# Graph layers on one core: products of the early y blocks move into the first stage

## The chip, the cores and the metric

The kernel runs on one core of a Trainium2 chip. The metric is the device time of the launch in microseconds, the median of the runs; lower is better. TensorE (PE), VectorE (DVE), ScalarE (ACT), GpSimd (POOL) and SyncE (SP) run their own instruction streams and meet at semaphores.

## The reference

6250 nodes with 128 features, 200,000 edges sorted by their target `dst`, and 128 attributes on every edge. Two layers, cut to what matters:

```
h = relu(layernorm(x));  xp = h @ W                      # 4 heads of 32
e = leaky_relu(a_s[src] + a_d[dst]);  m = segment_max(e, dst)
alpha = exp(e - m[dst]) / segment_sum(exp(e - m[dst]), dst)
x = x + relu(segment_sum(alpha * xp[src], dst) + bias)   # loops included

h = relu(layernorm(x));  edge_agg = segment_sum(attr @ We + be, dst)
x_comb = [h, edge_agg];  neigh = segment_sum(x_comb[src], dst)
x = x + relu((x_comb + neigh) @ W1 + b1) @ W2 + b2
```

The second layer's sum over neighbours is linear, so the kernel projects first: y = x_comb @ W1 (one row of 128 per node), and needs z = y + A y, where A counts the edges from each source to each target.

## The kernel before

**First stage.** The edges are taken in 87 groups of 2304 (18 columns of 128), some 72 target rows each; a group's window is the 128 rows from its first target on. `item(n, b, it)` exists for each engine and handles group n with buffers b = n mod 2; `pairs` and `groups` unroll two groups in a loop body. In one group POOL gathers 18 x 128 rows of a table by `src` (L816). DVE reads the logits from them (L1638), scans for segment maxima (L1643, L1664), builds one-hot selections; TensorE merges the peaks (L1161), looks up shifts (L1177), sums attributes (L1133) and, once DVE has scaled the gathered rows V (L1742), sums V (L1194). DVE and ScalarE finish the window of the group before in between (layernorm, projection to y), and SyncE stores it to `sums1`.

Beside it the kernel builds A. For each of a group's 18 columns TensorE makes an adjacency pair: two products of one-hot edge marks (L1123 and L1125) into one of three PSUM banks, which ScalarE copies to `adjE[b]` (`keep_adjacency`, L905, shown as L852). Columns 0 to 2, 3 to 5 and so on stand at fixed places between the other work; columns 9 to 14 stand behind the V products, 15 to 17 in the next group. `adjE[b]` holds, for the group's 128 target rows, a 128 x 49 table: sources are split in 49 blocks of 128 (`adjT[b][:, :, h]` is the block h, with sources on the partitions). SyncE stores it to `adj` in DRAM one group later (`store_adjacency`). Each engine runs its list in order; SyncE's list is written out by hand in `item`, L540 on.

**Second stage.** When all is stored, SyncE loads y from `sums1` in four chunks (`YCH`) and DVE and ScalarE split every block into three bf16 parts side by side (`y_part`), giving `yb` with 384 columns a block. Then 49 windows of 128 rows: SyncE loads the window's adjacency (three buffers, `load_adjacency`, 1568 KB), TensorE accumulates 49 products of 384 columns (L1248), DVE reduces the three parts (L1799) and adds y's own rows, loaded by `load_z` into `state` (L1803). TensorE transposes the window before at product 16 and projects it at product 32 (`transpose_z`, `project_z`), ScalarE applies the relu, DVE adds the residual (L1792), SyncE stores the output.

Behind it stands a general path for inputs whose rows a group's window doesn't cover (`uncovered`, from `flag`); it does not run for these inputs.

## Time and profile before

| | us |
|---|---|
| median of 3 runs (lowest, highest) | 3118.07 (3117.33, 3122.89) |
| profiled execution, its own time | 3102.13 |
| its span | 3100.2 |
| PE busy / DVE / ACT / POOL | 2043.0 / 1807.2 / 1085.6 / 1673.2 |
| mean granted TensorE clock | 0.764 |

Busy shares are means over the whole span, and the two stages differ, so most of what is read below is by stretch. In the slices a digit is a tenth of a slice of 77.5 us. Granted clock 1.00 stands for 2.4 GHz, 0.50 for 1.2 GHz, values between for a stretch that holds both. Times in a timeline are from the span's start.

### The profile page before, as it was taken

How to read it: one execution, taken by the hardware profiler on the slowest of the kernel's cores; microseconds unless marked ns; L12 is line 12 of the kernel's file. 1: busy time of each engine (PE TensorE's matmuls, PEld its weight loads, DVE VectorE, ACT ScalarE, POOL GpSimd, SP SyncE). 2: the span in 40 equal slices, each digit the busy share in tenths (PEclk: the TensorE clock that was granted, in tenths of full speed). 3: DMA queues.
4: the chain of work that ended last, by engine and by line, in shares of the span. 5: the costliest groups of instructions: out<-in, count | busy, mean ns of one | idle time of the engine just before them, and what ended most of it. 6: DMA issues, size and time to landing. Idle time of an engine off the chain costs nothing.

```text
span 3100.2 us, 64216 instructions
## 1 busy us (share of the span) xinstructions
PE 2043.0 (66%) x16208; PEld 1674.9 (54%) x16208; DVE 1807.2 (58%) x6198; ACT 1085.6 (35%) x2295; POOL 1673.2 (54%) x1626
## 2 busy tenths in 40 slices
PE   4365665665665655665656656656656656699998
PEld 3354554554554544554545545545545544588887
DVE  7566676665666666666666766766766766411111
ACT  3134344344434443443443443443444443300000
POOL 4566666666666666666666666666666666000000
PEclk8677777776777767777767777777777777799999
DMA  9855655655655555655556556556556555666654
GB/s 192 134 163 177 194 168 174 195 159 180 193 155 187 177 169 189 189 160 185 162 176 194 157 184 194 168 173 194 156 185 194 156 185 176 225 213 214 225 212 146
DMA packets 276907, 560.29 MB, mean 181 GB/s; under 512 B 113395, under 2 KB 211139, under 8 KB 248081
## 3 DMA queue, kind: packets, MB, share of 16 engines
q1 hardware_dynamic: 226763, 444.37, 42.5%
q0 software_dynamic: 50112, 115.56, 16.5%
q8 instruction: 12, 0.20, 0.0%
q14 instruction: 20, 0.16, 0.0%
HBM read 382.53 MB, written 177.22 MB: 181 GB/s over the span
## 4 chain that ended last, share of the span: by engine, by line
PE 41%; issue 20%; DVE 15%; DMA 9%; another core or an unknown queue 5%; SPq 3%; ACT 2%; POOL 2%; ACTq 1%; DVEq 1%; POOLq 0%
PE pv L1133 10%; PE pv L1248 9%; DMA big<-table,idx 8%; PE pv L1194 7%; PE pt L1248 4%; PE pt L1123 3%; PE pm L1161 2%; POOL big L816 2%; ACT xsb L852 2%; PE pa L1123 1%; DVE peaks L1513 1%; DVE tabb L1477 1%; PE pa L1177 1%; ACTq L905 1%
## 5 line engine op out<-in xcount | busy, mean ns | idle before, releaser
L816 POOL DMA_INDIRECT big<-table,idx x1566 | 1639.8, 1047 | 929.9 <-issue 414.2
L852 ACT ACTIVATE xsb<-pt 128x343 f32 x1042 | 477.8, 459 | 1213.3 <-PE pt L1125 567.1
L1133 PE MATMUL pv<-big 128*128 128x128 f32 x3132 | 523.6, 336 | 5.7 <-ACT big L852 3.5
L1133 PEld LDWEIGHTS pv<-big 128*128 128x128 f32 x3132 | 490.3, 246 | 36.1 <-issue 11.7
L1123 PE MATMUL pt<-tabb 128*128 128x343 bf16 x1042 | 400.0, 384 | 65.8 <-ACT xsb L852 36.5
L1194 PE MATMUL pv<-big 128*128 128x133 f32 x3132 | 391.3, 280 | 7.0 <-DVE big L1742 4.2
L1638 DVE COPY logit<-big 128x72 f32<-128x72 f32 x87 | 21.9, 252 | 608.6 <-DMA big<-table,idx 540.1
L1194 PEld LDWEIGHTS pv<-big 128*128 128x128 f32 x3132 | 367.8, 190 | 16.2 <-DVE big L1742 8.6
L1477 DVE TENSOR_TENSOR tabb<-iotah,keyp 128x2064 bf16<-128x2064 bf16 x261 | 319.7, 1225 | 0.0
L1142 PE MATMUL pm<-ident,pre 128*4 128x128 f32 x87 | 32.5, 374 | 433.9 <-DVE pre L1643 226.5
L1248 PE MATMUL pv<-big,xsb 128*128 128x384 bf16 (+1 forms) x1617 | 279.3, 330 | 18.5 <-DVE big L1779 18.5
L852 ACT ACTIVATE xsb<-pa 128x343 f32 x521 | 238.9, 458 | 95.0 <-ACT xsb L852 50.3
L1248 PEld LDWEIGHTS pv<-big,xsb 128*128 128x128 bf16 (+1 forms) x1617 | 230.4, 147 | 52.4 <-issue 21.4
L1142 PEld LDWEIGHTS pm<-ident,pre 128*4 128x4 f32 x87 | 7.2, 82 | 451.5 <-DVE pre L1643 236.4
L1742 DVE TENSOR_TENSOR big<-big,pm 128x768 f32<-128x768 f32 x261 | 233.4, 949 | 26.2 <-ACT pm L852 18.7
L1125 PE MATMUL pt<-tabb 128*128 128x49 bf16 x1041 | 224.9, 216 | 0.0
L1123 PE MATMUL pa<-tabb 128*128 128x343 bf16 x521 | 200.8, 385 | 28.3 <-issue 18.3
L1161 PE MATMUL pm<-peaks,selb 128*128 128x13 bf16 x1566 | 56.2, 174 | 228.8 <-DVE peaks L1513 143.7
L1123 PEld LDWEIGHTS pt<-tabb 128*128 128x128 bf16 x1042 | 114.9, 110 | 159.5 <-ACT xsb L852 63.1
L1161 PEld LDWEIGHTS pm<-peaks,selb 128*128 128x128 bf16 x1566 | 48.5, 105 | 261.2 <-DVE peaks L1513 157.2
L852 ACT ACTIVATE big<-selb 128x2304 f32<-128x2304 bf16 x87 | 184.1, 2116 | 1.0 <-DVE selb L1477 1.0
L852 ACT ACTIVATE fhT<-pt,b1s 128x128 f32<-128x128 f32 (+1 forms) x49 | 18.0, 367 | 388.6 <-PE pt L1225 388.6
(289 smaller groups left out, 2975.8 us busy)
## 6 DMA issues: line engine op xcount, KB each, us to landing
adj<-xsb SPq DMA_DIRECT2D x87, 1568.0 KB
big<-in_edge_attr_dram SPq DMA_DIRECT2D x87, 1152.0 KB
xsb<-adj SPq DMA_DIRECT2D x33, 1568.0 KB, 6.2
selb<-rel SPq DMA_DIRECT2D x87, 576.0 KB
tabb<-adj SPq DMA_DIRECT2D x16, 1568.0 KB, 6.2
big<-table,idx POOLq DMA_INDIRECT x1566
state<-sums SPq DMA_DIRECT2D x87, 130.5 KB
sums<-state SPq DMA_DIRECT2D x87, 130.5 KB
```

The source lines that it names most:

```text
L816: pool.indirect_dma_start(out=V[b][:, j, 0:rows], out_offset=None, in_=table, in_offset=bass.IndirectOffsetOnAxis(ap=index[b][:, j:j + 1], ...
L852: return nc.scalar.activation(out_, in_, func, **kw).then_inc(s(name), 1)
L905: _, at = nc.values_load_multi_w_load_instructions(offs[0:1, bass.DynSlice(n * OW + lo, hi - lo)], engines=[mybir.EngineType.Activation], ...
L1123: ins = nc.tensor.matmul(pab[c % 3], ohl[:, c, :], ohk[:, c, 0:KW], start=True, stop=alone)
L1125: ins = nc.tensor.matmul(pab[c % 3][:, 0:NB], ohl[:, (c - 1) % J, :], ohc[:, (c - 1) % J, 0:NB], start=False, stop=True)
L1133: ins = nc.tensor.matmul(sumA[b], SEL[b][:, j, :], AT[b][:, j, :], start=(j == 0), stop=(j == J - 1))
L1142: nc.tensor.transpose(tailT, pre1[:, :, J - 1], ident[:, :]).then_inc(s("tailT_b"), 1)
L1161: ins = nc.tensor.matmul(mg, selH[:, j, :], peaks[:, j, :], start=(j == 0), stop=(j == J - 1))
L1194: ins = nc.tensor.matmul(sumV[b], SEL[b][:, j, :], V[b][:, j, 0:TAB], start=(j == 0), stop=(j == J - 1))
L1248: ins = nc.tensor.matmul(pay[k][0:rows, 0:NK * C], adjT[k][:, 0:rows, h], yb[:, h, :], start=(h == 0), stop=(h == NB - 1))
L1477: return v.tensor_tensor(to.rearrange("p j (w e) -> p j w e", e=2), v_in, at, ALU.is_equal)
L1742: v.tensor_tensor(v4, v4, wps[:, js, :].rearrange("p j (h a) -> p j h a", a=1) .to_broadcast([128, QUART, H, F]), ALU.mult).then_inc(s("vw ...
```

## The change

The product of a group's adjacency with y is a sum over the 49 source blocks. Blocks 0 to 18 (`HB = 19`) of y are complete before group 42 (`EARLY`). The change:

- In groups 4 to 41 (stage "split") one of these blocks per pair of groups is loaded from `sums1` and split into its three parts, into `ybl`, in the free end of the table buffer.
- In groups 42 to 86 (stage "late") TensorE multiplies the adjacency rows of the group before with the 19 blocks, between the adjacency pairs 9 to 14: three products behind each, four behind the last. DVE reduces the three parts (`keep_products`) at the end of its item, SyncE stores them to a new table `zpart`. One more such step for group 86 stands behind the last group.
- In the second stage windows 24 to 48 (`WLATE = 24`) start at block 19; SyncE loads their rows of `zpart` too and DVE adds them. `yb` holds 30 blocks, loaded in three chunks. In these windows the transpose stands at product 13 of 30 and the projection at product 25 of 30; in the first 24 they stand at 13 and 25 of 49.
- `sums1` and `zpart` are zeroed whole during groups 0 and 1, where only the rows behind 6249 of `sums1` were zeroed in the prologue. Two conditions on the input are added to `flag`. Several small buffers share space, which changes no order of work.

```diff
+HB = 19
+EARLY = 2 * (HB + 2)
+WLATE = 24
-YCH = ((0, 13), (13, 25), (25, 37), (37, 49))
+YCH = ((19, 29), (29, 39), (39, 49))
...
+        def staged(eng, body):
+            for it in range(2):
+                for b in range(2):
+                    body(it * 2 + b, b, it, "plain")
+            for lo, hi, stage in ((2, EARLY // 2, "split"), (EARLY // 2, NG // 2, "late")):
+                with eng.Fori(lo, hi) as it:
+                    for b in range(2):
+                        body(it * 2 + b, b, it, stage)
+            body(NG - 1, 0, NG // 2, "late")
...                                                    # SyncE
+            def clear(ap, name):
+                sp.dma_start(ap.rearrange("(p q) c -> p q c", p=128),
+                             init[:, H:H + C].rearrange("p (a c) -> p a c", a=1).to_broadcast([128, NPAD // 128, C]))
+                    .then_inc(s(name), 16)
+            def load_block(n, h):
+                row = sp.value_load(blocks[0:1, bass.DynSlice(h, 1)], min_val=0, max_val=N - 1)
+                sp.wait_ge(s("y_out"), n * 16 - 16)
+                sp.dma_start(yst, sums1[bass.DynSlice(row, 128), :]).then_inc(s("yl0"), 16)
+            def store_products(n):
+                head = sp.value_load(heads[0:1, bass.DynSlice(n - 2, 1)], min_val=0, max_val=N - 1)
+                after(sp, s("zp_f"), n, 1)
+                after_dma(sp, s("zp_out"), n)
+                sp.dma_start(zpart[bass.DynSlice(head, 128), :], zps).then_inc(s("zp_out"), 16)
...
                 if not before_first:
                     store_residual(n - 1, base_before)
+                if stage == "split" and b == 0:
+                    load_block(n, it - 2)
                 if not (isinstance(n, int) and n < 2):
                     store_projected(n - 2, base_of(n - 2))
+                if isinstance(n, int) and n < 2:
+                    clear((sums1, zpart)[n], ("y_out", "zp_out")[n])
                 if not before_first:
                     store_adjacency(n - 1, 1 - b)
+                if stage == "late":
+                    store_products(n + 1)
...
             store_adjacency(NG - 1, 0)
             store_projected(NG - 1, base)
+            store_products(NG + 1)
...
                     load_z(w + 1)
+                    if late or (static and w == WLATE - 1):
+                        load_products(w + 1, LASTW if static and w == NB - 2 else 128)
...                                                    # ScalarE; DVE has the subtractions in between
+            def split_block(h, k):
+                if k == 0:
+                    act.wait_ge(s("yl0"), h * 16 + 16)
+                    a(ybl[:, bass.DynSlice(h, 1), 0:C]..., yst, ACT.Copy, "ys0")
+                else:
+                    act.wait_ge(s("ysr"), h + 1)
+                    a(ybl[:, bass.DynSlice(h, 1), C:2 * C]..., yst, ACT.Copy, "ys1")
                 a(thruT[:, :], thruP, ACT.Copy, "thru_c")
+                if stage == "split" and b == 1:
+                    split_block(it - 2, 0)
...
                     normalise_window(n - 1)
+                if stage == "split" and b == 1:
+                    split_block(it - 2, 1)
...                                                    # TensorE
+            def row_products(n, b, lo=0, hi=HB):
+                if lo == 0:
+                    ...
+                    pe.wait_ge(s("ys2"), HB)
+                    after(pe, s("zp_f"), n, 2)
+                for h in range(lo, hi):
+                    ins = nc.tensor.matmul(rpP, adjT[b][:, :, h], ybl[:, h, :], start=(h == 0), stop=(h == HB - 1))
+                if hi == HB:
+                    ins.then_inc(s("rp_b"), 1)
...
-                if not is_extra:
+                if stage == "late":
+                    for c in range(9, 15):
+                        adjacency(n, c, c + 1)
+                        row_products(n + 1, 1 - b, 3 * (c - 9), 3 * (c - 9) + 3 if c < 14 else HB)
+                elif not is_extra:
                     adjacency(n, 9, 15)
...
-                for h in range(NB):
+                first_h = HB if late else 0
+                for h in range(first_h, NB):
...
-                        if h == 16:
+                        if h == first_h + 13:
                             transpose_z(w - 1, (k - 1) % 3)
-                        if h == 32:
+                        if h == first_h + 25:
                             project_z(w - 1)
...                                                    # DVE
+            def keep_products(n):
+                after(dve, s("rp_b"), n, 1)
+                after_dma(dve, s("zp_out"), n)
+                v.tensor_reduce(zps, rpP.rearrange("p (k c) -> p c k", k=NK), AX.X, ALU.add).then_inc(s("zp_f"), 1)
                 between(newton_square, 0)
+                if stage == "split" and b == 1:
+                    split_block(it - 2, 0)
...
                         .to_broadcast([128, QUART, H, F]), ALU.mult).then_inc(s("vw_b"), 1)
+                if stage == "split" and b == 1:
+                    split_block(it - 2, 1)
                 if not is_extra:
                     edge_marks(n, 2)
                     if not (isinstance(n, int) and n == NG - 1):
                         edge_marks(n + 1, 0)
+                if stage == "late":
+                    keep_products(n + 1)
...
-                dve.wait_ge(s("z_load"), w * 16 + 16)
+                dve.wait_ge(s("z_load"), w * 32 + (32 - 16 * WLATE) if late else w * 16 + 16)
+                if late:
+                    v.tensor_tensor(state[0:rows, 0:C], state[0:rows, 0:C], zq[0:rows, :], ALU.add)
+                        .then_inc(s("fin"), 1)
```

## Rows read from the trace of the kernel before

**Rows 1.** The page, part 2: the span in 40 slices.

```profile
PE   4365665665665655665656656656656656699998
...
PEclk8677777776777767777767777777777777799999
```

**Rows 2.** Windows, second stage: PE, PEld, DVE, ACT, POOL busy; PEclk, DMA share, GB/s.

```profile
2694.00:2900.00 206.00, 206.00 (x1294) 180.87 (x1292) 28.54 (x75) 8.92 (x25) 0.00 (x0) 1.00 0.61 217
```

**Rows 3.** Timeline, one second-stage window; start, duration us, engine, line, operation.

```profile
2906.63 0.56 DVE L1799 TENSOR_REDUCE cols<-pt 128x128 f32<-128x384 f32 x1 [2.37 <-PE pt L1248]
2906.78 0.33 SPq L593 DMA_DIRECT2D tabb<-adj  x1
2907.29 0.29 DVE L1803 TENSOR_TENSOR cols<-cols,state 128x128 f32<-128x128 f32 x1
2907.75 0.33 SPq L597 DMA_DIRECT2D state<-sums  x1
...
2914.92 0.56 DVE L1799 TENSOR_REDUCE cols<-pv 128x128 f32<-128x384 f32 x1 [2.37 <-PE pv L1248]
```

**Rows 4.** All reads of the gathered logits (L1638) from group 42 on.

```profile
L1638 DVE COPY logit<-big x45: 219/221/455, 1349.1 to 2633.2; 128x72 f32<-128x72 f32 x45
...
  DMA big<-table,idx: 280.4, 40
```

**Rows 5.** Timeline behind the V products of group 47.

```profile
1520.20 0.31 PE L1123 MATMUL pt<-tabb 128*128 128x343 bf16 x1
...
1523.02 0.94 POOL L816 DMA_INDIRECT big<-table,idx  x1 [0.30 <-issue]
...
1523.14 0.32 PE L1123 MATMUL pt<-tabb 128*128 128x343 bf16 x1 [0.29 <-issue]
...
1528.42 0.22 DVE L1638 COPY logit<-big 128x72 f32<-128x72 f32 x1 [8.10 <-DMA big<-table,idx]
...
1529.12 0.38 PE L1142 MATMUL pm<-ident,pre 128*4 128x128 f32 x1 [5.24 <-DVE pre L1643]
```

**Rows 6.** Source views, 2700:3100: the loads of sums (L597) and adjacency (L593).

```profile
DMA to landing us min/median/max: 1.7/5.4/5.8
...
DMA to landing us min/median/max: 6.0/6.2/6.6
```

**Rows 7.** Timeline, the last window's products and reduces.

```profile
3080.77 0.56 DVE L1799 TENSOR_REDUCE cols<-pt 128x128 f32<-128x384 f32 x1 [2.37 <-PE pt L1248]
...
3091.16 0.56 DVE L1799 TENSOR_REDUCE cols<-pv 106x128 f32<-106x384 f32 x1 [3.12 <-PE pv L1248]
```

**Rows 8.** Windows view behind the V products of group 47, and on.

```profile
1520.40:1523.20 2.80, 1.56 (x11) 0.52 (x10) 0.00 (x0) 1.98 (x5) 1.46 (x3) 1.00 1.06 389
1523.20:1528.40 5.20, 0.56 (x3) 0.13 (x3) 0.00 (x0) 1.64 (x4) 3.98 (x5) 0.71 0.92 354
1528.40:1535.40 7.00, 3.17 (x31) 1.93 (x32) 6.74 (x29) 2.85 (x4) 5.52 (x5) 0.50 0.30 72
```

**Rows 9.** The prologue and the first groups: DVE, SyncE's issues, and a windows view.

```profile
117.54 0.06 DVE L1751 MEMSET cont<- 128x4 f32 x1 [21.12 <-DMA peak<-tabb]
...
153.23 0.36 SPq L509 DMA_DIRECT2D sums<-state  x1
...
172.05 0.36 SPq L526 DMA_DIRECT2D adj<-xsb  x1
...
44.00:62.00 18.00, 9.40 (x65) 7.79 (x64) 16.45 (x35) 5.80 (x14) 16.19 (x14) 0.88 1.11 254
```

**Rows 10.** Between the stages: the first adjacency load and the first products.

```profile
2662.64 0.35 SPq L593 DMA_DIRECT2D xsb<-adj  x1
...
2679.91 13.68 PE L1248 MATMUL pv<-big,xsb 128*128 128x384 bf16 x65 [18.51 <-DVE big L1779]
```

**Rows 11.** Windows view from logits to the end of V, groups 43 and 44.

```profile
1378.80:1399.00 20.20, 15.59 (x143) 13.09 (x144) 18.38 (x64) 8.74 (x18) 11.90 (x13) 0.75 0.49 147
1405.00:1429.50 24.50, 17.91 (x144) 15.61 (x145) 19.14 (x67) 8.92 (x18) 14.33 (x15) 0.63 0.44 118
```

More of the change, by code:

```diff
@@ L355, in triples, with windows @@
                     body(it * 3 + k, k, it)
+        def windows(eng, body):
+            for k in range(3):
+                body(k, k, 0, False)
+            for lo, hi, late in ((1, WLATE // 3, False), (WLATE // 3, NB // 3, True)):
+                with eng.Fori(lo, hi) as it:
+                    for k in range(3):
+                        body(it * 3 + k, k, it, late)
+            body(NB - 1, 0, NB // 3, True)
         PAST = (NG // 2 + NX // 2 + 1, NG // 2 + NX // 2)
@@ L956, in _ @@
             act.wait_ge(s("masks"), 11)
-            groups(act, item)
+            staged(act, item)
             keep_adjacency(NG - 1, 0, 15, 18)
@@ L1755, in _ @@
             edge_marks(0, 0)
-            groups(dve, item)
+            dve.sem_inc(s("zp_f"), EARLY)
+            staged(dve, item)
             m = NG - 1
@@ L1868 @@
 PADS = 0
-for _wd in (DL, H, ST, C):
+for _wd in (DL, H, ST):
     PADS += -(-((NPAD - N) // 75 * _wd) // (ST - C - H))
```

173 lines of the change are left out of this document (109 added, 64 removed).

## The prediction

> **What bounds the kernel now.** I read the page's slices first [rows 1]: the first 34 show PE at four to seven tenths, the granted clock at seven, and the last five show both at nine. So there are two programs in one, and the change takes TensorE work out of the second (full) and puts it into the first (with holes).
>
> The second stage. The windows view of 206 us of it [rows 2] has PE busy in all 206, granted clock 1.00 (2.4 GHz), DMA share 0.61 at 217 GB/s. The timeline of one window [rows 3] shows DVE's reduce at 2906.63 and again at 2914.92: 8.29 us per window, in which 16, 16 and 17 products stand back to back with a transpose and a projection. 2.76 us for 17 gives 0.1625 us a product; 49 x 0.1625 = 7.96, and 0.33 for the two other steps makes the 8.29. The period is TensorE's alone.
>
> The first stage. The 45 reads of the gathered logits from group 42 on go from 1349.1 to 2633.2 us [rows 4], 44 steps of 29.18 us; before 40 of them DVE stood idle for a gather, 280.4 us, so 7.0 us each, from about the end of the V products on. The timeline of one such gap [rows 5]: the V products end at about 1520.4, six adjacency pairs follow, the first at 1520.20 and the last at 1523.14, in steps of some 0.6 us (ScalarE's evacuations), TensorE then does one small transpose and waits until 1529.12. What ends the gap is the last gather, issued at 1523.02, after V, and read at 1528.42. So work put behind V is beside a wait for DMA, if it ends early enough.
>
> **The change part by part.**
>
> Second stage, products removed. Windows 24 to 48, 25 of them, keep 30 of 49 products. For 24 full windows TensorE alone would need 30 x 0.1625 + 0.33 = 5.21 us. What is late next? First the DMA: a window moves 1.606 MB of adjacency (its row is still loaded whole) and now four pieces of 0.066 MB in place of three, 1.87 MB; at 217/0.61 = 356 GB/s that is 5.25 us. Then a loop through the queue [rows 3, 6]: the adjacency load of window w+3 is issued when w's products end, the load of the earlier sums for w+1 behind it, and both land together, 6.2 and 5.4 us after their issues, so the small load waits for the big one. Before this fitted into 8.29. After it: the projection of w-1 now stands 5 products before w's end (17 before), so SyncE reaches the adjacency load some 0.75 us after w's products instead of 0.28 (its residual and output issues are in front, each as long as those in rows 3, with what lies between); it lands 6.2 later, the sums and the new products' load 0.4 behind it, DVE adds twice (0.29 each, 0.9 with the waits and the hand-over), and TensorE, which waits for that in the middle of w+2, has 17 products and the two steps left (3.1). That is 0.75 + 6.2 + 0.4 + 0.9 + 3.15 = 11.4 us for two windows, 5.7 each, if the landing stays at 6.2; it was measured with a queue that starts empty, so some of it goes when loads follow closely. I take 5.6, ends 5.2 (TensorE) and 5.9: 24 x (8.29 - 5.6) = 64.6 us saved, ends 74 and 57. The last window has 106 rows and slower products [rows 7]: 10.39 us between reduces, (10.39 - 0.33)/49 = 0.205 each, so 19 fewer save 3.9. The new addition at the very end costs 0.4. Together -68.1.
>
> The Trainium skill weighs on this term. Its page DMA: Bandwidth & Descriptors (Specifications) gives about 358 GB/s of HBM per core as the limit; rows 2 work out to the same 356 at full share, while a 2.8 us stretch shows 389 [rows 8]. By the page's figure 1.87 MB need at least 5.2 us, which leaves the 5.6 standing and rules out only a hope of less than TensorE's own time.
>
> First stage, products added. 45 groups get 19 products of 384 columns each, three behind each of five adjacency pairs and four behind the sixth. The clock is 1.00 in the stretch behind V [rows 8], so they cost 0.1625 as in the second stage: 3.09 us; a pair has 392 columns, 0.16 us, so all of it ends 4.1 us behind V, against 3.1 now. Each step (0.16 + 0.49 = 0.65) is about as long as ScalarE's now, so ScalarE ends when it did. Queued behind: DVE waits at the end of its item for the nineteenth product, reduces 384 columns (0.56, as L1799 in rows 3), and only then writes the four columns that TensorE's first transpose of the next group wants, which ScalarE copies. From 1520.4 that puts the reduce's end at about 1525.2, the transpose at 1525.6 and ScalarE's copy at 1526.2; the logits come at 1528.4 and the copy is wanted at 1529.1 [rows 5]. Hidden, by about 2.9 us here and by some 2 in a mean group (a gap of 7.0 against 8.1 here). SyncE waits for the products at the end of its item too; behind it stand only next group's stores, which wait for sums some 3 us after the logits. The 64 KB store that follows has a queue that is emptying. Cost of the 45 groups: 0.1 each for the odd short gap, 4; bounds: without the cover the whole 3.1 + 0.7 each, +170, and below nothing by the clock (a rival). Value taken near the hidden end, since 40 gaps are 280 us together [rows 4], a few short ones can hide among them, and the products with what follows need 5.2.
>
> First stage, the 19 splits. In 19 of the groups 4 to 41 a 64 KB load, two ScalarE copies and two DVE subtractions of 128x128 are added. The second subtraction is behind the V scaling, where DVE has only marks to make for later. The first stands just before DVE reads the merged peaks, 0.29 us (as L1803, which has the same shape [rows 3]) in the chain from peaks to shifts to lookups; ScalarE's two copies (0.4) each go in front of evacuations. I take 0.29 a group, 5 us; ends 0 and 0.7 x 19 = 13.
>
> First stage, the clearing of two tables. Two DMAs of 3.28 MB in 512 B pieces, behind groups 0 and 1. The stretch of the first stage's own filling of sums ran at 254 GB/s with all engines taken [rows 9]: 13 us each. The first is issued near 141 and drains before SyncE's next issue at 153.23 [rows 9]; the second is in front of adjacency store 0 (172.05), which would land near 190, while ScalarE wants to overwrite that buffer's partner at about 190. I take 2 us, ends 0 and 15. Six or seven more tiny DVE steps in the prologue are free: DVE then stands idle 21 us for a DMA [rows 9]. More copies of the loop bodies: 1 us.
>
> Between the stages. Now: first adjacency load 2662.64, the chunk loads behind it, first product 2679.91, and window 0 done near 2690.9 (65 products in 13.68, 16 of them window 1's), 3 us more than its own 8, since four chunks' splitting paces it [rows 10]. The change puts the last group's 19 products and SyncE's wait for their sum in front of that load; TensorE has been idle before it, and is at half clock then as behind the gap of rows 8: 19 x 0.325 = 6.2 us, + 0.7 for the reduce, from about 2661, and the load goes out near 2668.8, 6 us later. Against it: window 0 can start with 19 blocks that are ready, the chunks are three of 10 blocks in place of four of 12 or 13 (1.3 MB less, split in six smaller steps of DVE in place of eight). From landing near 2677.5 the last half is split near 2688 and ten products end at 2690. I take -1, ends -6 and +6.
>
> Sum: -68.1 + 4 + 5 + 2 + 1 - 1 = -57 us. The profiled execution has 3102.13 us (span 3100.2 and 1.9 around it), 16 below the median of the runs, 3118.07; it would become 3045, and the median **3061 us**.
>
> **The rivals.**
>
> (a) The small loads don't follow so closely, and the serial loop binds: sum written, next sums loaded (5.4 us from issue [rows 6]), products' load issued behind it (0.45), two additions (0.9). That gives 6.9 us a window whatever TensorE does. For it: the next load waits for the last addition, since both use one buffer. Against: most of the 5.4 is the wait behind the adjacency load, which is issued earlier. It would save 24 x 1.4 = 34 instead of 65: 3092 us.
>
> (b) The clock gains. Between V and the logits it falls back to 1.2 GHz, 0.71 on the mean [rows 8], and 0.50 follows. The stretch from logits to V took 20.2 us at 0.75 and 24.5 us at 0.63 in two neighbouring groups [rows 11], 0.36 us per hundredth. If the longer run of products lifts it by two hundredths in 45 groups, 32 us more go: 3029 us. Against: 3 us of idleness stay between the products' end and the logits, and in the 7 us behind these TensorE is busy for 3.2 [rows 8]. The Trainium skill, TensorE: Matmul & The Clock Gate (What's actually happening), says that activity releases the throttle and idleness restores it; rows 8 agree, and by its rule the added work could only help.
>
> (c) Slower than before: the products do not fit into the gap. Place: DVE's wait at the end of its item, in front of the columns for the next group. If TensorE runs that stretch at 1.2 GHz, 19 x 0.325 + 6 x 0.33 = 8.2 us, the reduce 0.7 and the columns 0.35 make DVE free 9.2 us behind V, 2.2 past the mean logits at 7.0; 45 x 2.2 = 99 against the 61 saved elsewhere (57 and the 4 counted for these groups): 3156 us. It decides from 61/45 = 1.4 us of delay a group, so from products that end 7.3 us behind V. Against: 1.00 in that stretch [rows 8].
>
> (d) The early blocks are not final in time, or the switch at window 24 does not hold for these edges, and the long fallback runs, hundreds of us. A group has 2304 edges, about 72 rows at 32 edges a row; group 2h+2 begins at row 144h+144, past block h's end at 128h+128, and group 41 at about 2952, before row 3072. It holds; 1 in 100.
>
> **How the numbers follow.** Forecast with its own range 3045 to 3080: 0.62. (a) 0.16, (b) 0.09, (c) 0.07, (d) 0.01; some loss that eats the whole gain and ends near 3118: 0.05. No change means within 0.2%, 6 us. Faster: 0.62 + 0.16 + 0.09 + 0.01 of the last = 0.88; same 0.03; slower 0.09. The range takes in (a) and half of (b): 3036 to 3100.
>
> **What would show it.** Late windows: reduces 5.6 us apart, 5.2 if no queue binds, 6.9 in (a), with a wait of PE's transpose for DVE's addition. Groups from 42: still 29.2 us from logits to logits, the last product about 4.1 us behind V, DVE's reduce about 5, and its idle time before the logits shorter but there. Groups 4 to 41: 0.1 to 0.3 us longer. First product of the second stage near 2676 plus what the first stage shifted. The forecast is wrong if the period from group 42 grows by over 0.5 us, or if the late windows stay above 6.3.

## The result, and the profile after

The changed kernel takes 3104.24 us (median of 20 runs, 3090.88 to 3119.57), the kernel before in its own 20 runs 3116.67: a ratio of 0.9967, 95% interval 0.9954 to 0.998. By the medians it is 12 us faster; I had forecast 57 and a range that ended at 3100.

The page's slices answer to [rows 1]: the last slices of PE fell from 9 to 8 and 7 in the late windows, and the granted clock of the first stage's second half rose from 7 to 7 and 8.

```profile
span 3107.0 us, 65764 instructions
...
PE   4356656656656656657676676767666666779988
...
PEclk8667777767777767777787877778787878789999
...
L1741 DVE TENSOR_REDUCE hb<-pc 128x128 f32<-128x384 f32 x46 | 25.6, 558 | 327.6 <-remote 161.5
```

Only the stretches between landmarks tell where the time is: first logits, logits of groups 4, 42 and 86, first reduce of the second stage, reduce of window 23, last reduce, end. Worked out from the timelines of the two traces, in us:

| stretch | before | after | forecast | measured |
|---|---|---|---|---|
| to the first logits | 126.2 | 133.3 | 0 | +7.1 |
| groups 0 to 3 | 114.3 | 114.5 | +2 | +0.2 |
| groups 4 to 41 | 1108.6 | 1113.6 | +6 | +5.0 |
| groups 42 to 85 | 1284.1 | 1335.7 | +4 | **+51.6** |
| last logits to first reduce | 57.8 | 62.3 | -1 | +4.5 |
| windows 1 to 23 | 190.7 | 191.9 | 0 | +1.2 |
| windows 24 to 48 | 209.4 | 148.4 | -68 | -61.0 |
| last reduce to the end | 9.1 | 7.3 | 0 | -1.8 |

The second stage. A late window in the timeline, against [rows 3]:

```profile
3035.03 0.56 DVE L1931 TENSOR_REDUCE cols<-pv 128x128 f32<-128x384 f32 x1 [0.42 <-PE pv L1351]
...
3035.88 0.33 SPq L651 DMA_DIRECT2D xsb<-adj  x1
...
3037.17 0.29 DVE L1935 TENSOR_TENSOR state<-state,hb 128x128 f32<-128x128 f32 x1 [1.58 <-DMA hb<-zpart]
3037.49 0.29 DVE L1939 TENSOR_TENSOR cols<-cols,state 128x128 f32<-128x128 f32 x1
3037.84 0.14 PEld L1326 LDWEIGHTS pt<-ident,cols 128*128 128x128 f32 x1 [1.08 <-DVE cols L1939]
...
3041.20 0.56 DVE L1931 TENSOR_REDUCE cols<-pt 128x128 f32<-128x384 f32 x1 [0.42 <-PE pt L1351]
```

Two windows take 11.98 us (the next reduce is at 3047.01). The loop through the queue that I forecast is there to be read: the adjacency load goes out 0.85 us behind the reduce, the load of the kept products lands last, DVE adds twice, and the weight load of TensorE's transpose waited 1.08 us for that. The 24 intervals from window 23 on are 5.91 us on the mean (5.6 forecast), the last one 6.53 (10.39 before [rows 7]).

The late groups. The logits from group 42 on, against [rows 4]: 1335.7 us for 44 groups, 30.36 us each in place of 29.18, and the wait for gathers in front of them is gone (28.7 us in place of 280.4).

```profile
L1762 DVE COPY logit<-big x45: 209/220/448, 1361.4 to 2697.1; 128x72 f32<-128x72 f32 x45
...
  DMA big<-table,idx: 28.7, 17
```

Two such groups, by ScalarE's timeline behind V, whose products end at 1835.9 and 2016.1. Each row is the copy of one adjacency pair and so a clock for TensorE, which makes a pair and three products between two of them.

```profile
1836.29 0.46 ACT L922 ACTIVATE xsb<-pt 128x343 f32 x1 [1.35 <-PE pt L1207]
1836.93 0.46 ACT L922 ACTIVATE xsb<-pa 128x343 f32 x1 [0.18 <-issue]
1837.63 0.46 ACT L922 ACTIVATE xsb<-pt 128x343 f32 x1 [0.24 <-PE pt L1207]
1838.33 0.46 ACT L922 ACTIVATE xsb<-pt 128x343 f32 x1 [0.24 <-PE pt L1207]
1839.03 0.46 ACT L922 ACTIVATE xsb<-pa 128x343 f32 x1 [0.24 <-PE pa L1207]
1839.73 0.46 ACT L922 ACTIVATE xsb<-pt 128x343 f32 x1 [0.24 <-PE pt L1207]
...
2016.42 0.46 ACT L922 ACTIVATE xsb<-pt 128x343 f32 x1 [0.69 <-PE pt L1207]
2017.13 0.46 ACT L922 ACTIVATE xsb<-pa 128x343 f32 x1 [0.24 <-issue]
2018.04 0.46 ACT L922 ACTIVATE xsb<-pt 128x343 f32 x1 [0.45 <-issue]
2019.50 0.46 ACT L922 ACTIVATE xsb<-pt 128x343 f32 x1 [1.00 <-PE pa L1207]
2020.94 0.46 ACT L922 ACTIVATE xsb<-pa 128x343 f32 x1 [0.99 <-PE pt L1207]
2023.11 0.46 ACT L922 ACTIVATE xsb<-pt 128x343 f32 x1 [1.71 <-remote]
```

In the first group the steps are 0.70 us, as forecast. In the second they are 0.91, 1.46, 1.44 and 2.17. The records of the products themselves show nothing of it: in both the last one is recorded 4.4 us behind V, at a granted clock of 1.00. Here are the slow group's other engines, and its windows (columns as in [rows 2]):

```profile
2019.64 0.85 PE L1220 MATMUL pc<-tabb,xsb 128*128 128x384 bf16 x4
...
2026.05 0.56 DVE L1741 TENSOR_REDUCE hb<-pc 128x128 f32<-128x384 f32 x1 [11.02 <-remote]
...
2026.90 0.37 PE L1233 MATMUL pm<-ident,thru 128*4 128x128 f32 x1 [6.40 <-issue]
2026.92 0.22 DVE L1762 COPY logit<-big 128x72 f32<-128x72 f32 x1
```

```profile
2018.00:2022.00 4.00, 2.50 (x18) 1.67 (x16) 0.00 (x0) 1.37 (x3) 2.95 (x4) 1.00 0.98 397
2022.00:2026.80 4.80, 0.00 (x0) 0.00 (x0) 0.69 (x3) 0.46 (x1) 3.72 (x4) 0.63 0.34 83
```

The last product is recorded at 2020.49 and DVE's reduce, which waits for it, begins at 2026.05; the logits wait for the reduce. Over the 44 groups the reduce ends 7.10 us behind V on the mean (forecast 5), and up to 10.8. So the step that failed is the cover of the 45 late groups: the products and the reduce, forecast to be hidden in front of the logits, in most groups end behind the gathers (DVE still waits for one in 17 of 45). The theories differ in what made the products late.

### The profile page after: what moved, and what is told of

Its sections match the earlier page's. It is cut to its first block, busy times and chain, and to the rows that moved or that the text cites. A ratio compares the mean times of both kernels' runs of the same rounds, so it can differ in the third digit from the quotient of the medians.

```text
span 3107.0 us, 65764 instructions
## 1 busy us (share of the span) xinstructions
PE 2096.8 (67%) x16607; PEld 1717.8 (55%) x16607; DVE 1845.5 (59%) x6312; ACT 1080.6 (35%) x2331; POOL 1669.7 (54%) x1626
## 4 chain that ended last, share of the span: by engine, by line
PE 36%; issue 21%; DVE 16%; DMA 10%; another core or an unknown queue 7%; SPq 3%; ACT 2%; POOL 1%; ACTq 1%; DVEq 1%; POOLq 0%
PE pv L1228 10%; PE pv L1289 6%; DMA big<-table,idx 6%; PE pv L1351 4%; DMA hb<-zpart 4%; PE pt L1205 3%; PE pc L1220 2%; DVE tabb L1585 2%; PE pt L1351 2%; PE pm L1256 2%; ACT xsb L922 2%; PE pa L1205 1%; POOL big L886 1%; PE pa L1272 1%
## 5 line engine op out<-in xcount | busy, mean ns | idle before, releaser
L1741 DVE TENSOR_REDUCE hb<-pc 128x128 f32<-128x384 f32 x46 | 25.6, 558 | 327.6 <-remote 161.5
L1220 PE MATMUL pc<-tabb,xsb 128*128 128x384 bf16 x874 | 198.4, 339 | 0.0
L1351 PE MATMUL pv<-big,xsb 128*128 128x384 bf16 (+1 forms) x990 | 176.8, 331 | 3.5 <-DVE big L1911 3.5
L1205 PEld LDWEIGHTS pt<-tabb 128*128 128x128 bf16 x1042 | 114.5, 110 | 110.6 <-ACT xsb L922 38.2
```

Source lines behind the costliest of these rows:

```text
L1205: ins = nc.tensor.matmul(pab[c % 3], ohl[:, c, :], ohk[:, c, 0:KW], start=True, stop=alone)
L1220: ins = nc.tensor.matmul(rpP, adjT[b][:, :, h], ybl[:, h, :], start=(h == 0), stop=(h == HB - 1))
L1351: ins = nc.tensor.matmul(pay[k][0:rows, 0:NK * C], adjT[k][:, 0:rows, h], part, start=(h == first_h), stop=(h == NB - 1))
```

## The experiments

Theory A: in these groups the store of the adjacency buffer reads, behind V, the same buffer whose columns the products take as weights, and the two contend. Rival B: TensorE itself is slower than its records. Rival E: DVE's in-order wait is what costs. The expectations also name rival C, the gathers of the next group, and rival D, the place of the products between the pairs. Theory F says that the groups 4 to 41 pay for the block's load in front of the adjacency store, its rival G that they pay for the load and the splitting themselves; the new order between the stages is about another of the smaller terms.

A warning ahead of the numbers. The kernel before took 2829 to 2860 us in three of the sets of runs below, and 3173 to 3176 in two; in the first comparison it took 3117. One chip was met in both conditions, so it is the condition of a chip at the time and not the chip. Each set has its own runs of the kernel before, and ratios are to those; a set is named by them, "the 2832 set".

**The 2832 set.** The adjacency store moved: behind the store of the products, in the late groups only; or up to 8 us behind the logits, in all groups, in the changed kernel and in the kernel before. e_other_weights gives the 19 products a constant tile as weights, so it leaves out what they are for, and keeps their number, their order and the store.

```
 # e_store_late                                # e_store_early, e_before_early
-    if not before_first:                          store_sums(n - 1, base_before)
-        store_adjacency(n - 1, 1 - b)             store_peak(n, b, base)
     if stage == "late":                      +    if not before_first:
         store_products(n + 1)                +        store_adjacency(n - 1, 1 - b)
+    if not before_first:                     ...
+        store_adjacency(n - 1, 1 - b)        -    if not before_first:
                                              -        store_adjacency(n - 1, 1 - b)
 # e_other_weights
-    nc.tensor.matmul(rpP, adjT[b][:, :, h], ybl[:, h, :], ...)
+    nc.tensor.matmul(rpP, identH[:, :], ybl[:, h, :], ...)
```

> In the groups from 42 the store of an adjacency buffer is put on SP's queue behind the store of the products, so no DMA reads that buffer while TensorE reads it for the 19 row products. Theory A (the products stall because the DMA store and the weight reads of the same buffer contend in SBUF): DVE's reduce of the products ends at 5.1 to 5.5 us behind V in nearly all groups (mean 7.1 in the changed kernel, up to 10.8), and the groups from 42 take at most 29.6 us (30.36). Rival B (TensorE itself gets slower there, whatever DMA does) and rival D (the products' place between the pairs): the reduce still ends at 7.1 on the mean, with the same groups past 9. Rival C (it is the gathers of the next group, not the store): the same as B. The store itself, issued 5 us later, may now press on the next group's first transfers: up to 0.5 us a group, with the period then not better although the reduce is early.

> The 19 row products of a late group take a constant 128x128 tile as weights in place of the adjacency buffer's strided columns; count, order and the store are left as they are (what is computed for the rows is then another thing). Theory A in its narrow form (two readers of the one buffer, strided weight columns against the DMA store): the reduce ends 5.1 to 5.5 us behind V in nearly all groups, periods under 29.6 us. Rival B and rival D: no change, 7.1 us on the mean. A wider form of A (any TensorE reading slows when the DMA store runs) gives 7.1 as well, so this run parts the narrow form from the rest.

> The changed kernel, with every adjacency store moved up on SP's queue to right behind the store of the group's peaks, some 8 us behind the logits, where the DMA queues of SP are busy under 10 per cent of the time. Theory A: nothing stores an adjacency buffer behind V any more, so the reduce ends near 5.2 us behind V and the groups from 42 take 29.2 us or less: 44 groups by 1.18 us, 52 us less than the changed kernel, 3052 us; the gathers of the next group also share the DMA engines with less behind V, worth 0 to 1 us a group more in all 87 groups. Rivals B and D: products as late as before; only what the gathers gain, 0 to 40 us. If the stored 1.5 MB now delays the small loads in the middle of the group, the logits-to-V time of 22.35 us grows and the kernel is slower than the changed one.

> The kernel before with the same move of the adjacency store alone. It has no row products, so theory A gives it nothing from them: 0 to 1 us a group from the gathers that land earlier behind V (V to logits 7.22 us), so 3030 to 3117 us. If it gains as much as the changed kernel with the same move does against the changed kernel, the gain is the gathers' and not the products'.

Measured: e_store_late 2742.94 (one run); e_other_weights 2802.56 (one run); e_store_early 2683.77, ratio 0.9472 (0.9451 to 0.9493); e_before_early 2717.19, ratio 0.9591 (0.9569 to 0.9613). In the three that have products the reduce ends at 5.12, 4.89 and 5.12 us behind V on the mean and never past 5.42. Each of them moves the store or replaces the weights, so it looked like theory A in its narrow form. But the changed kernel as it is, in the next two sets, is as punctual (5.12, never past 5.42): in this condition nothing is late, and the set decides nothing between A and B. It showed something not looked for: the place of the store is worth 115 us to the kernel before, and about 120 to the changed one, if that takes 0.99 of before here as in the next two sets. V to logits is 5.08 to 5.55 us with the early store and 5.32 with the late one, where the kernels with the store behind V have 6.3 to 6.7: there it goes out beside the last gathers.

**The 2860 set.** The changed kernel as it is; two of the 19 products only (17 left out, so the sums are not complete); the reduce behind the next group's selection; and that together with the early store.

```
 # e_two_products                    # e_reduce_next, e_early_next
 for h in range(lo, hi):             -    if stage == "late":                  # end of item
+    if h == 0 or h == HB - 1:       -        keep_products(n + 1)
         ins = nc.tensor.matmul(      ...     select(n, b, extra_group)
             rpP, ...)               +    if stage == "late" and ... n != EARLY:
                                     +        keep_products(n)
```

> The changed kernel as it is, a second time, for comparison: the four kernels run before this one met a chip on which the kernel before takes 2832 us and not 3117. On such a chip the groups' transfers land sooner. Theory A (the stall of the products comes with the adjacency store's reads of the same buffer while the DMA engines are all taken) says the reduce of the products ends on the mean 5.1 to 5.5 us behind V wherever the DMA share behind V is under 0.9, and past 6.5 where it is over 1. The ratio to the kernel before: 0.985 on a chip as fast as that (the 57 us of the prediction less the 4 us that the changed kernel lost between the stages), 0.997 on one like the first.

> Of the 19 row products of each late group only the first and the last are computed (products with 17 y blocks are left out); everything else of the changed kernel stays: reduce, stores, clears, the shorter late windows. Where the products' own time on TensorE is what the groups from 42 pay, their period falls to that of the groups 4 to 41 (within 0.2 us). Where the reduce, the store of the products and the loads are what they pay, the period stays above by what the changed kernel has.

> DVE's reduce of a late group's products goes from the end of its group to behind the selection of the next, so the copy of the logits no longer waits for it. Rival E (the in-order wait on DVE is what costs, not the delay of TensorE): logits come when the gathers land, V to logits falls to that of the groups 4 to 41, and the groups from 42 take 0.5 to 1 us less than in the changed kernel on the same chip. Theory A in the form that a late TensorE is the cost: the transpose behind the products is still late, and under 0.3 us a group comes back.

> The changed kernel with both edits: adjacency stores early in the group, and the reduce of the products behind the next group's selection. With the store moved, the reduce (5.12 us behind V) was the last to end in front of the logits in the groups from 42 (DVE idle 0.2 us; V to logits 5.55 us, where the kernel before with the same move has 5.08). Without it there, V to logits falls by up to 0.47 us, 44 groups: 10 to 20 us less than the changed kernel with the store moved alone (0.947 of before there), so 0.941 of the kernel before. If it takes 0.947 again, something else ends as late (TensorE, whose pairs and products end 4.37 us behind V, with the next transposes behind them).

Measured: r_after 2834.82, ratio 0.9909 (0.9877 to 0.994), where 0.985 was expected; e_two_products 2824.82 (one run); e_reduce_next 2870.34 (one run); e_early_next 2749.57, ratio 0.96 (0.9569 to 0.9631). The changed kernel alone, in its late groups: every step 0.70, the reduce at 5.12 us.

```profile
1732.49 0.56 DVE L1741 TENSOR_REDUCE hb<-pc 128x128 f32<-128x384 f32 x1 [4.21 <-PE pc L1220]
...
1734.61 0.22 DVE L1762 COPY logit<-big 128x72 f32<-128x72 f32 x1 [1.39 <-DMA big<-table,idx]
```

(These rows are of the 2829 set's run of the same kernel; V ended at 1728.0.) DVE stands idle 1.39 us for the gather behind the reduce: the cover that I had forecast. Leaving out 17 of 19 products takes 26.46 us a group to 26.33, so here the products cost 0.1 us, not 1.2. Rival E fell: with the reduce moved, V to logits went from 6.69 to 6.59 us only, and logits to V from 19.77 to 20.63. I put that down to the 0.56 us, which now stand in the chain of the next group's scans; no run shows it apart. The combination, forecast at 0.941, got 0.96. The same reason can be a part of that only: its groups 4 to 41, which have no reduce to move, took 25.47 us against 25.12 in e_store_early, a run of the other set.

**The 2829 set.** Both kernels, and two repeats.

> The kernel before once more, for its profile on the same chip as the others of this call; time 1.000 of itself. What is wanted of it: first logits and the periods of the groups 4 to 41 and 42 to 85. If the changed kernel's 7 us before the first logits are the code's, the first logits come 7 us earlier here than in the changed kernel on this chip; if they are the chip's or the run's, they come within 1 to 2 us of each other.

> The changed kernel again beside a profile of the kernel before. Theory A on a chip with short groups (under 27 us): products never stalled, reduce ends 5.1 us behind V, ratio 0.985 to 0.992. On a chip with groups of 29 us: reduce on the mean 7 us behind V, up to 10.8, groups from 42 a full microsecond longer than those before them, ratio 0.997.

> Adjacency store behind the products' store in the groups from 42, now beside the changed kernel on the same chip. Theory A: no stalled product anywhere (reduce ends 5.1 us behind V in each group, whatever the chip), and groups from 42 shorter than in the changed kernel, by 1.2 us or more. Rivals B and D: on a chip where the changed kernel stalls, this one stalls too.

> Row products with a constant tile as weights (what they compute is another thing), beside the changed kernel. On a chip where that stalls: the narrow form of theory A (two readers of one buffer) says no stall here; the wide form (the matmuls' reads slow whenever the DMA engines are full) says the same stall. On a chip where the changed kernel does not stall it tells only the period: within 0.3 us of it in the groups from 42.

Measured: r_before 2837.89 (one run); r_after_2 2797.45, ratio 0.9905 (0.9872 to 0.9938); e_store_late_2 2737.5; e_other_weights_2 2787.6 (one run each). Reduces at 5.12, 5.12 and 4.89 us again. The late groups of e_store_late_2 took 24.76 us where the changed kernel beside it has 26.05. Theory A had asked for 1.2 us or more, but no product was late in either kernel: most of the gain is in V to logits (5.32 against 6.38), which I put down, as above, to the store beside the last gathers. Here both kernels have a profile on one chip: logits from 126.4 and 125.6 us on. The 7.1 us in front of the first logits were a chip's or a run's (the four kernels of the 2860 set have 135.5 to 137.9), not the code's. Stretch by stretch the change does: groups 0 to 3 +3.3, groups 4 to 41 +12.9, groups 42 to 85 +2.2, between the stages +3.6, windows 1 to 23 +1.2, windows 24 to 48 -65.5, the end -1.9. That adds up to 45 us between the two profiled executions, where the medians of the runs are 31 apart, so some us of it are scatter between single executions. Logits of both, kernel before first:

```profile
L1638 DVE COPY logit<-big x45: 220/221/419, 1226.0 to 2369.9; 128x72 f32<-128x72 f32 x45
...
  DMA big<-table,idx: 291.4, 45
```

```profile
L1762 DVE COPY logit<-big x45: 220/221/446, 1241.4 to 2387.6; 128x72 f32<-128x72 f32 x45
...
  DMA big<-table,idx: 49.5, 45
```

26.00 us a group before and 26.05 after, with 242 us of waiting for gathers used up: the forecast of +4 for these groups holds here.

What was larger, groups 4 to 41, is for two thirds (8.6 of 12.9 us) in the even ones, which load a y block (V to logits 7.02 us; odd 6.37; in the kernel before 6.49 and 6.34). The odd ones, which split the block, have 0.20 us more from logits to V. SyncE's timeline of an even and an odd group, logits at 658.2 and 685.6:

```profile
675.32 0.38 SPq L553 DMA_DIRECT2D resid<-dlog  x1
676.62 0.33 SPq L563 DMA_DIRECT2D hb<-sums  x1
677.94 0.36 SPq L558 DMA_DIRECT2D sums<-pick  x1
679.35 0.35 SPq L575 DMA_DIRECT2D adj<-xsb  x1
...
702.40 0.43 SPq L553 DMA_DIRECT2D resid<-dlog  x1
703.70 0.36 SPq L558 DMA_DIRECT2D sums<-pick  x1
705.03 0.33 SPq L575 DMA_DIRECT2D adj<-xsb  x1
```

The adjacency store goes out 21.2 us behind the logits where the block is loaded and 19.4 where it is not (20.5 and 19.0 on the mean of 19 groups each). The block's load (L563) does not wait for the y store, which was issued a group earlier: from the issue in front of it to its own are 1.30 us, and from that to the next 1.32, and in the odd group, which has no such load, the steps are the same 1.30 and 1.33. So it is one more issue in SyncE's row, in front of which the code reads its address, that holds up the large store.

**The 3176 set.** The changed kernel; the block's load behind the adjacency store; the early store with a new order between the stages; each product made twice.

```
 # e_block_behind                                 # e_early_end: early store, block load later, and
-    if stage == "split" and b == 0:                   store_projected(NG - 1, base)
-        load_block(n, it - 2)                    -    store_products(NG + 1)
     ...                                          -    load_adjacency(0, 0)
         store_adjacency(n - 1, 1 - b)                 ...                  # the three y chunks
+    if stage == "split" and b == 0:              +    sp.wait_ge(s("rp_b"), NG + 1)
+        load_block(n, it - 2)                    +    for k in range(3):
 # e_double_products: per product                 +        load_adjacency(k, k)
+    nc.tensor.matmul(rpP, ..., stop=False)            load_z(0); load_residual(0)
     ins = nc.tensor.matmul(rpP, ...)             +    store_products(NG + 1)
```

> The changed kernel again, to have it beside the others of this call, and in case the chip is one like the first (the kernel before at 3117 us). On a chip like the three since (before at 2829 to 2860): steps between the late groups' adjacency copies 0.70 us throughout, ratio 0.991. On one like the first: theory A (store against products in SBUF) has fallen in any case if TensorE is as late in the stretches without an adjacency store (the 18 look-up matmuls, 4.5 us from the sum of the shift to DVE's reduce, 3.5 us on the other chips).

> In the even groups 4 to 40 the load of an early y block goes behind the adjacency store on SP's queue instead of ahead of it. Theory F: the block's wait for the y store of the group before holds SP for 1.6 us, the 1.5 MB store starts and lands 0.8 to 1 us later, and the last gathers of the next group with it: V to logits 7.02 us in even groups against 6.37 in odd ones and 6.49 in the kernel before. Then here even groups fall to 26.3 us and the kernel takes 8 to 12 us less than the changed one. Rival G: it is the load's 64 KB, ACT's and DVE's splitting, or the code, and the even groups stay at 26.8 us (within 3 us of the changed kernel).

> The changed kernel with all adjacency stores early in the group (0.947 of before in its first run), the y block's load behind the projected store, and between the stages the last store of products put behind the first loads of the second stage, with the y chunks first, the three adjacency windows behind them, and a wait on the products' own semaphore ahead of the one that overwrites their buffer. In the changed kernel SP waits 4.1 us between the last store of y and that of the products, with the first loads of the second stage behind it. Expected: last logits to first reduce 60.5 us down to 56.5 or less, and the whole 0.945 of the kernel before or less. If the first window instead waits for its adjacency, which now comes behind the y chunks, that distance stays at 60.

> Each of the 19 row products of a late group is made twice (38 matmuls, the sum doubled). Added columns 19 x 384 at full clock are 3.0 us: products end 7.4 us behind V and the reduce at 8.1, which is past where logits came (6.4), so the groups from 42 grow by 1.5 to 2.5 us. If a longer stretch of TensorE work is itself what brings the slower steps seen in the first profile (rival B as a matter of load), the steps between the adjacency copies double from 1.2 to 2.4 us somewhere and the reduce ends past 9. If it is that chip's alone, they stay at 1.2.

Measured: r_after_3 3173.01, ratio 0.9984 (0.9956 to 1.0011); e_block_behind 3168.12, ratio 0.9973 (0.9949 to 0.9997); e_early_end 3154.96, ratio 0.9912 (0.9885 to 0.994); e_double_products 3262.19 (one run). The late products are back: in the changed kernel the reduce ends 8.60 us behind V on the mean (up to 13.4) and the late groups take 31.58 us. e_early_end decides on theory A. Its products are as late as ever (reduce at 8.11 us on the mean, up to 13.4). In SyncE's timeline of one late group the adjacency store goes out 10 us before V ends (1591.4), and SyncE issues nothing between the small y store at 1590.39 and the store of the products:

```profile
1581.13 0.02 SPq L575 DMA_DIRECT2D adj<-xsb  x1
...
1604.59 0.33 SPq L569 DMA_DIRECT2D zpart<-hb  x1
```

ScalarE's copies of the pairs behind V:

```profile
1592.38 0.46 ACT L921 ACTIVATE xsb<-pa 128x343 f32 x1 [0.24 <-PE pa L1206]
1593.09 0.46 ACT L921 ACTIVATE xsb<-pt 128x343 f32 x1 [0.25 <-PE pt L1206]
1595.29 0.46 ACT L921 ACTIVATE xsb<-pt 128x343 f32 x1 [1.74 <-PE pt L1206]
1597.45 0.46 ACT L921 ACTIVATE xsb<-pa 128x343 f32 x1 [1.71 <-remote]
1599.62 0.46 ACT L921 ACTIVATE xsb<-pt 128x343 f32 x1 [1.71 <-remote]
```

The windows view of the slow stretch:

```profile
1594.00:1600.00 6.00, 1.76 (x13) 1.12 (x10) 0.00 (x0) 1.29 (x3) 4.48 (x6) 0.99 0.20 52
```

And DVE, which waits for the last product:

```profile
1603.86 0.56 DVE L1740 TENSOR_REDUCE hb<-pc 128x128 f32<-128x384 f32 x1 [13.83 <-remote]
```

A pair and three products take 2.2 us in place of 0.70 while the DMA engines are busy for 0.20 of the time, DVE is idle and the granted clock reads 0.99. Theory A is refuted: in the last 2.2 us steps no large store is under way, and what moves, 52 GB/s, is the next group's gathers. What is left is rival B, a TensorE that works slower than its records say. Rival D alone can't be it, since in the 2829 and 2860 sets the products stand in the same place and are on time. Whether the gathers of rival C have a part in the slowness stays open: they run beside the late products in every trace, and no run is without them.

The double products confirm that it is TensorE's work that is paid. Their late groups grew by 2.1 us over the changed kernel's, inside the 1.5 to 2.5 expected, but from products far later than the 8.1 us of that working: in one group the first steps behind V are 1.00, 1.19 and 1.19 us, about what six products and a pair need at full rate, then 1.98 and 2.88; the reduce ends at 13.38 us on the mean and the late groups take 33.66 us. With none, 19 and 38 products a group took 29.8 (groups 4 to 41), 31.58 and 33.66 us: 0.09 to 0.11 us for each product, no matter how large the hole behind V is. And the early store, worth over 4% in the 2832 set, brought some 0.7% here, with the new order between the stages: V to logits fell in the groups 4 to 41 from 6.86 to 5.17 us, as there, but logits to V grew from 22.96 to 24.88, and the period went from 29.8 to 30.0. Groups of some 30 us whatever is moved about inside them fit a bound on TensorE's work per time; no run with less of it was made in this condition.

**The 3173 set.** The same two kernels again.

> The same kernel as e_early_end, whose run met a chip on which the kernel before takes 3176 us; there the reduce of the products ended 8.1 us behind V although no adjacency store ran within 6 us of V, and theory A fell by that. Where the kernel before takes 2830 to 2860 us: steps of 0.70 us between the adjacency copies in every late group, reduce 5.1 us behind V, groups of 25.1 us, last logits to first reduce 58 us or less, ratio 0.945 or less. Where it takes 3100 to 3200 us: reduce on the mean past 8 us, ratio 0.99 again; then what the early stores give is lost to the slower TensorE.

> The same kernel as e_block_behind, of which the first run told nothing: V to logits in the groups 4 to 41 spread by more than the 0.6 us in question there. Where the kernel before takes 2830 to 2860 us, theory F: V to logits in the even groups 4 to 40 falls from 7.0 to 6.4 us and the whole by 8 to 12 us, ratio 0.987 (0.9905 for the changed kernel). Rival G (the load and the splitting themselves): even groups stay at 7.0.

Measured: e_early_end_2 3158.29, ratio 0.9964 (0.9934 to 0.9995); e_block_behind_2 3169.66, ratio 0.9992 (0.9966 to 1.0018). Reduces 8.01 and 8.08 us behind V, late groups 31.16 and 31.38. The condition asked for was not met, so the edit tells nothing of theory F: with the block's load behind the store V to logits was 7.7 us in the even groups of the 3176 set and 7.9 in those of this one, in the odd ones 7.2 and 7.4, and 6.6 and 7.1 in the changed kernel of the 3176 set, all in a condition where TensorE is late. Two runs of the 2832 set say more. In e_store_early the block's load no longer stands in front of the adjacency store. Against e_before_early, the same move without the change, its even groups 4 to 40 took 24.90 us for 25.07, as theory F has it; but the odd ones took 25.35 for 24.43, and the 38 groups together 14.1 us more, no less than the 12.9 above. So the loss of these groups does not go with the place of the load, one profile each. That the first loads of the second stage wait for the last store of products is shown only in part: with the new order the last logits stand 59.3 and 57.3 us in front of the first reduce, where e_block_behind has 61.6 and 61.7 in the same sets, 2.3 and 4.4 less where 4 was expected.

## Why the prediction was wrong, point by point

*Second stage.* Right in mechanism and nearly in size: 61.0 us gained in the first comparison and 65.5 in the 2829 set, 68.1 forecast. The late windows take 5.91 and 5.72 us against 5.6: the serial loop has its wait, and rival (a) with 6.9 did not come (the terms written there add up to 6.75).

*The 19 products behind V.* This is the step that failed: +4 forecast, +51.6 measured. The working took the granted clock of 1.00 behind V [rows 8] for TensorE's speed, had the products end 4.1 us behind V and the reduce at about 5, and gave rival (c) 0.07 by it. Measured, the reduce ends at 7.10 on the mean and up to 10.8, where the logits came at 7.2 before. What (c) described is what came: products slower than 0.1625 us, DVE's wait at the end of its item, the logits behind it. Only its cause was misnamed: no record shows 1.2 GHz there, and by (c)'s own prices a pair and three products would take 1.3 us at it, where steps of 2.2 were seen. With 1.18 us a group in place of 2.2 it ate most of the gain and not all. In the 2829 set the same step is right to 2 us.

It could have been read in the trace of before, in a row that I passed over. DVE's reduce of the look-up products waited for something that the profile could not name:

```profile
L1725 DVE TENSOR_REDUCE lks<-pa 128x144 f32<-128x432 f32 x34 | 20.6, 607 | 27.4 <-remote 27.4
```

```profile
L1725 DVE TENSOR_REDUCE lks<-pa 128x144 f32<-128x432 f32 x38 | 22.7, 597 | 0.0
```

Both rows are of the grouped view from 231 to 1226 us, the first of the kernel before as profiled for the prediction, the second of its run in the 2829 set: 0.8 us of idleness in each of 34 groups, and none. In one group 18 small products are recorded from 1388.03 to 1388.69, and the reduce of their sums begins at 1391.19, where in the other condition it follows its marks at once:

```profile
1388.03 0.66 PE L1177 MATMUL pa<-node,selb 128*128 128x24 bf16 x18
...
1391.19 0.61 DVE L1725 TENSOR_REDUCE lks<-pa 128x144 f32<-128x432 f32 x1 [0.91 <-remote]
```

TensorE was done some 2.4 us behind its own record before anything was added.

*The clock.* Rival (b) forecast gains by a better clock in the long run from logits to V. The granted clock did rise there (0.69 to 0.71 in the late groups, 0.72 to 0.77 in the 2829 set), yet the stretch got longer by 0.4 us in the first comparison and stayed (19.72 and 19.67) in the 2829 set. The Trainium skill, TensorE: Matmul & The Clock Gate (What's actually happening), has activity release the throttle, and I took from it that added work can only help. For the granted clock the traces agree; for the time they don't: in the 3176 set 19 more products a group cost 2.1 us.

*Splits and clears.* Groups 4 to 41 were forecast at +6 with the loop bodies and were +5.0 and +12.9. DVE's 0.29 us in the chain came near: the odd groups, which split, took 0.23 us more each in the 2829 set. What the working left out is the even groups' 0.45 us. There the block's load stands in front of the adjacency store on SyncE's queue, and the 1.5 MB go out 1.5 us later. That is the time of one more issue and not the wait for a y store that the expectation of e_block_behind names. Whether the later store is what the even groups pay is not shown: with the store early they paid nothing, but then the odd ones paid 0.92 us, and why stays open. The clears, with the groups 0 to 3, were +2 forecast, +0.2 and +3.3 measured.

*Between the stages.* Forecast -1, measured +4.5 and +3.6. Of the two sides the loss was right, SyncE's wait for the last products in front of the first load; the gain from 19 blocks that are ready did not make up for it.

*Rival (d)* did not come: the path for uncovered inputs, hundreds of us, did not run.

## What to carry to other kernels

Holes of one engine are not free room by their length alone: take the engine's real ends from those who wait for it (the copies and reduces behind it), not from its own records, and when a wait is put down to nothing that the profile knows, ask first whether the engine in front is slower than recorded. Time a change in more than one condition of the chip: this one was worth 0.9% where TensorE kept its pace, 0.3% in the first comparison, and nothing clear of the scatter in the 3176 set. And place large stores by the stretch in which their queue's neighbours are quiet: moving one store from behind V to 8 us behind the logits gave 4.1% to the kernel before, and 5.3% together with the change, in the one condition, 0.4 to 0.9% together with the change and the new order between the stages in the other. So with the store early the changed kernel beats the kernel before in both conditions, though no one version of it was run in both.

## What the runs showed of the hardware

One and the same kernel took 2832 and 3176 us on one chip, at two times. In the slower condition fp32 products of 128 columns are recorded at 337 ns in place of 322, which explains little; the larger part is time that the records don't hold: a pair and three products, 0.70 us where all is well, take 1.45, 2.2 us and more, at a granted clock of 0.99 to 1.00. The second stage is spared: its full windows took 8.34 us in the changed kernel in either condition, with TensorE busy all the time at 1.00. What differs is that DVE, ScalarE, GpSimd with its gathers and fp32 products are at work in the first stage and nearly absent in the second. Which of them brings it on, and what sets the condition of the chip, stays open; no run here was made to tell.
